# An order of work written as a table: VectorE's operations with two SBUF operands moved to PSUM, the score mask to ScalarE and GpSimd

## The reference, cut to what matters

```python
x = _layernorm(x + _L0_gnn_ref(x, adj, ...))   # attention, 12 heads, with an adjacency mask
x = _layernorm(x + _L1_gnn_ref(x, adj, ...))   # 2 graph convolutions
x = _layernorm(x + _L2_gnn_ref(x, adj, ...))   # 2 directed convolutions
x = _layernorm(x + _L3_gnn_ref(x, adj, ...))   # attention, 12 heads, adjacency as a bias
...
scores = scores + beta * adj_e
scores = jnp.where(adj_e > 0, scores, -9000000000000000.0)
probs = jax.nn.softmax(scores, axis=-1)
...
u = u_left * adj_tri + u_left * diag_mask + u_right * jnp.swapaxes(adj_tri, 1, 2)
delta_exp_u = jnp.exp(u) * adj
attention = delta_exp_u / (jnp.sum(delta_exp_u, axis=2, keepdims=True) + 1e-10)
```

## Time and profile before

| | |
|---|---|
| time, median of 3 runs | 2729.16 us (2726.61 to 2732.68) |
| profiled execution | 2730.39 us, span 2728.5 us |
| TensorE busy | 2582.3 us, 95% |
| VectorE busy | 2077.7 us, 76% |
| ScalarE busy | 2046.5 us, 75% |
| GpSimd busy | 2117.1 us, 78% |
| granted TensorE clock, mean | 0.986 |

### The profile page before, as it was taken

How to read it: one execution, slowest core, us unless ns; L and a number is a source line. 1 busy time by engine, 2 the same in 40 slices (tenths; PEclk the granted TensorE clock), 3 DMA queues, 4 the chain that set the end, 5 groups by cost and what they waited for, 6 DMA issues and landing times.

```text
span 2728.5 us, 90881 instructions
## 1 busy us (share of the span) xinstructions
PE 2582.3 (95%) x33728; PEld 1930.4 (71%) x33728; DVE 2077.7 (76%) x7848; ACT 2046.5 (75%) x5716; POOL 2117.1 (78%) x3211
## 2 busy tenths in 40 slices
PE   5899999999999999999999999999999999999995
PEld 4667777776777777777777777777777777777763
DVE  6677877777877777777777777777787777887774
ACT  6667777777777777777777777777777777787775
POOL 6577878778778788778787788888787787887774
PEclk9899999999999999999999999999999999999997
DMA  7734544445444544444454454444454544454433
GB/s 182 164 62 78 90 86 83 91 84 93 81 87 80 91 91 80 90 91 80 87 94 80 88 93 80 90 91 79 88 94 84 86 88 79 85 96 82 78 61 74
DMA packets 809952, 243.18 MB, mean 89 GB/s; under 512 B 768688, under 2 KB 808752, under 8 KB 809520
## 3 DMA queue, kind: packets, MB, share of 16 engines
q1 hardware_dynamic: 801056, 222.42, 45.5%
q10 hardware_dynamic: 8464, 14.94, 1.8%
HBM read 35.92 MB, written 12.58 MB: 18 GB/s over the span
## 4 chain that ended last, share of the span: by engine, by line
PE 45%; POOL 18%; DVE 16%; ACT 7%; DMA 6%; issue 6%; SPq 1%; DVEq 0%; POOLq 0%; ACTq 0%
PE bank L921 7%; PE bank L923 6%; PE bank L922 6%; PE bank L912 5%; PE bank L913 5%; PE bank L914 5%; DMA region<-region 5%; POOL region L717 3%; DVE region L1091 3%; POOL ab L733 3%; PE bank L995 3%; ACT region L832 2%; POOL region L706 2%; PE bank L951 2%; POOL region L733 2%
## 5 line engine op out<-in xcount | busy, mean ns | idle before, releaser
L912 PE MATMUL bank<-region,w_hi 128*128 128x128 f16 x3960 | 686.0, 220 | 35.0 <-DMA region<-region 25.0
L913 PE MATMUL bank<-region,w_hi 128*128 128x128 f16 x3960 | 685.6, 220 | 0.0
L914 PE MATMUL bank<-region,w_lo 128*128 128x128 f16 x3960 | 685.4, 220 | 0.0
L921 PE MATMUL bank<-w_hi,region 128*128 128x384 f16 x1815 | 593.9, 327 | 11.4 <-DMA region<-region 6.1
L923 PE MATMUL bank<-w_hi,region 128*128 128x384 f16 x1815 | 593.2, 327 | 0.0
L922 PE MATMUL bank<-w_lo,region 128*128 128x384 f16 x1815 | 593.1, 327 | 0.0
L717 POOL TENSOR_TENSOR region<-region 128x512 f16<-128x512 f32 x330 | 385.2, 1167 | 220.6 <-ACT region L838 219.2
L832 ACT ACTIVATE region<-region,small 128x128 f32<-128x128 f32 x1320 | 419.8, 390 | 133.1 <-DVE small L1091 73.2
L912 PEld LDWEIGHTS bank<-region,w_hi 128*128 128x128 f16 x3960 | 390.0, 98 | 63.3 <-issue 26.4
L1091 DVE CUSTOM_DVE_ANT_0 region<-bank,mask 128x128 f32<-128x128 f32 x1320 | 304.4, 285 | 134.5 <-PE bank L951 123.2
L913 PEld LDWEIGHTS bank<-region,w_hi 128*128 128x128 f16 x3960 | 389.9, 98 | 23.8 <-issue 16.5
(11 more groups left out here) (229 smaller groups left out, 7795.8 us busy)
## 6 DMA issues: line engine op xcount, KB each, us to landing
region<-region SPq DMA_TRANSPOSE x715, 3.1
last_unit<-w_dram ACTq DMA_DIRECT2D x19, 576.0 KB, 6.0
x<-x_dram SPq DMA_DIRECT2D x55, 192.0 KB, 2.5
out_dram<-region SPq DMA_DIRECT2D x55, 192.0 KB, 2.2
adj<-adj_dram SPq DMA_DIRECT2D x55, 64.0 KB, 2.3
mask<-adj_t_dram SPq DMA_DIRECT2D x55, 64.0 KB, 2.0
rows<-rows_dram ACTq DMA_DIRECT2D x5, 576.0 KB, 4.3
last_unit<-last_unit SPq DMA_TRANSPOSE x117, 3.1
```

The source lines that it names most:

```text
L912: pe.matmul(dst, lhsT=w_hi[:, w, k, cols], rhs=t_hi[u][:, k, :], start=(k == 0), stop=False)
L913: pe.matmul(dst, lhsT=w_hi[:, w, k, cols], rhs=t_lo[u][:, k, :], start=False, stop=False)
L914: last = pe.matmul(dst, lhsT=w_lo[:, w, k, cols], rhs=t_hi[u][:, k, :], start=False, stop=(k == DT - 1))
L921: pe.matmul(dst, lhsT=t_hi[u][:, k, :], rhs=w_hi[:, w, k, :], start=(k == 0), stop=False)
```

## The change

No instruction of VectorE reads two operands from SBUF any more, the preparation of the weights aside. `masks` is split: ScalarE multiplies the adjacency by minus beta, GpSimd makes the barred entries and adds both. `divide` keeps its inverse in the PSUM bank of the last `attend` (attend 2 or 5), the first attention's quotient lies there too, and `residual` 0 reads it from there; so this bank is held until `residual` 0 or `divide` 1. `u_gcn` multiplies its halves one by one, the second in its bank, and adds from there. A small denominator of `inner` moves to the bank as well. `PARTS`, `SHIFTED` and `PERIOD` have new numbers throughout, so that all lists and banks change.

```diff
-PERIOD = 20.1080
+PERIOD = 20.0041
...
-    (VECTOR, "masks", 0): (2.743, 0.600, 0.900, ((SYNC, "load", 0),), ()),
+    (POOL, "masks", 0): (-115.045, 1.020, 1.100, ((SCALAR, "masks", 0),), ()),
+    (SCALAR, "masks", 0): (-94.836, 0.190, 0.300, ((SYNC, "load", 0),), ()),
...
-           "scores": lambda s: (VECTOR, "scores", s), "attend": lambda s: (SCALAR, "attend", s),
+           "scores": lambda s: (VECTOR, "scores", s), "attend": lambda s: {DT - 1: (VECTOR, "residual", 0), 2 * DT - 1: (VECTOR, "divide", 1)}.get(s, (SCALAR, "attend", s)),
...
-        u_pair = [a[:, 0:2 * N].rearrange("p (a n) -> p a n", n=N) for a in score_at]
+        u_left = [a[:, 0:N] for a in score_at]
...
         def inner_of(i, k):
+        def denom_of(made):
+            return made[:, PD - 1:PD]
...
+            def masks(i, k):
+                u = i % UNITS
+                pool.wait_ge(*loaded.at(i, "in"))
+                pool.tensor_scalar(score[u][:, 3, :], adj[u], 0.0, -MASKED, ALU.is_le, ALU.mult).then_inc(gpsimd_done.of(i), 1)
+                pool.wait_ge(*gpsimd_done.at(i, "barred"))
+                pool.wait_ge(*scalar_done.at(i, "minus beta"))
+                pool.tensor_tensor(mask_bias[u], mask_bias[u], score[u][:, 3, :], ALU.add).then_inc(gpsimd_done.of(i), 1)
...
+            def masks(i, k):
+                u = i % UNITS
+                if (k, i) == first(SCALAR, "masks"):
+                    act.wait_ge(beta_loaded, 16)
+                    act.activation(minus_beta[:, :], beta[:, :], ACT.Copy, scale=-1.0).then_inc(minus_beta_made, 1)
+                    act.wait_ge(minus_beta_made, 1)
+                act.wait_ge(*loaded.at(i, "in"))
+                act.activation(mask_bias[u], adj[u], ACT.Copy, scale=minus_beta[:, 0:1]).then_inc(scalar_done.of(i), 1)
...
+                    elif read_by == "divide":
+                        pe.wait_ge(*mixed_out.at(j, "o", n))
...
-            def masks(i, k):
-                u = i % UNITS
-                if (k, i) == first(VECTOR, "masks"):
-                    dve.wait_ge(beta_loaded, 16)
-                    dve.tensor_scalar(minus_beta[:, :], beta[:, :], -1.0, None, ALU.mult).then_inc(minus_beta_made, 1)
-                    dve.wait_ge(minus_beta_made, 1)
-                dve.wait_ge(*loaded.at(i, "in"))
-                dve.tensor_scalar(mask_bias[u], adj[u], 0.0, -MASKED, ALU.is_le, ALU.mult).then_inc(numbers.of(i), 1)
-                dve.wait_ge(*numbers.at(i, "mask"))
-                dve.scalar_tensor_tensor(mask_bias[u], adj[u], minus_beta[:, 0:1], mask_bias[u], ALU.mult, ALU.add)\
-                   .then_inc(numbers.of(i), 1)
...
             def scores(i, s):
-                    dve.wait_ge(*numbers.at(i, "mask and beta"))
+                    dve.wait_ge(*gpsimd_done.at(i, "mask"))
...
             def divide(i, k):
+                held = bank("attend", DT * k + DT - 1, i)
+                inverse = held[:, PD - 2 * H:PD - H]
+                dve.wait_ge(*max((scalar_done.at(i, "o", DT * k + t) for t in range(DT)), key=lambda at: at[1]))
+                dve.reciprocal(inverse, o_un[u][:, :, HD]).then_inc(numbers.of(i), 1)
+                    not_low = held[:, PD - H:PD]
-                    dve.tensor_scalar(flag[u], low[u], 0.0, None, ALU.not_equal).then_inc(numbers.of(i), 1)
+                    dve.tensor_scalar(not_low, low[u], 0.0, None, ALU.not_equal).then_inc(numbers.of(i), 1)
-                    dve.scalar_tensor_tensor(flag[u], top[u], 0.0, flag[u], ALU.not_equal, ALU.max).then_inc(numbers.of(i), 1)
-                dve.wait_ge(*max((scalar_done.at(i, "o", DT * k + t) for t in range(DT)), key=lambda at: at[1]))
-                dve.reciprocal(inv[u], o_un[u][:, :, HD]).then_inc(numbers.of(i), 1)
-                if k:
-                    dve.wait_ge(*numbers.at(i, "inverse", k))
-                    dve.tensor_tensor(inv[u], inv[u], flag[u], ALU.mult).then_inc(numbers.of(i), 1)
+                    dve.scalar_tensor_tensor(flag[u], top[u], 0.0, not_low, ALU.not_equal, ALU.max).then_inc(numbers.of(i), 1)
+                    dve.wait_ge(*numbers.at(i, "row is not 0", k))
+                    dve.tensor_tensor(inverse, inverse, flag[u], ALU.mult).then_inc(numbers.of(i), 1)
-                dve.tensor_tensor(o[u].rearrange("p (h c) -> p h c", c=HD), o_un[u][:, :, 0:HD],
-                                  inv[u].unsqueeze(2).broadcast_to([128, H, HD]), ALU.mult).then_inc(mixed_out.of(i), 1)
+                dst = o[u] if k else held[:, 0:D]
+                dve.tensor_tensor(dst.rearrange("p (h c) -> p h c", c=HD), o_un[u][:, :, 0:HD],
+                                  inverse.unsqueeze(2).broadcast_to([128, H, HD]), ALU.mult).then_inc(mixed_out.of(i), 1)
             def u_gcn(i, layer):
-                dve.tensor_tensor(u_pair[u], bank("u_gcn", layer, i)[:, 0:2 * N].rearrange("p (a n) -> p a n", n=N), mask_pair[u], ALU.mult)\
-                   .then_inc(numbers.of(i), 1)
-                dve.wait_ge(*numbers.at(i, "masked", layer))
-                dve.tensor_tensor(e_of(i, "u_gcn", layer), u_pair[u][:, 0, :], u_pair[u][:, 1, :], ALU.add).then_inc(mixed_out.of(i), 1)
+                left, right = (bank("u_gcn", layer, i)[:, n * N:(n + 1) * N] for n in range(2))
+                dve.tensor_tensor(u_left[u], left, mask_pair[u][:, 0, :], ALU.mult).then_inc(numbers.of(i), 1)
+                dve.tensor_tensor(right, right, mask_pair[u][:, 1, :], ALU.mult).then_inc(numbers.of(i), 1)
+                dve.wait_ge(*numbers.at(i, "right masked", layer))
+                dve.tensor_tensor(e_of(i, "u_gcn", layer), right, u_left[u], ALU.add).then_inc(mixed_out.of(i), 1)
...
-                dve.tensor_scalar(col(u, DENOM3), made[:, D:D + 1], 1e-10, 1e-3, ALU.add, ALU.mult).then_inc(numbers.of(i), 1)
+                dve.tensor_scalar(denom_of(made), made[:, D:D + 1], 1e-10, 1e-3, ALU.add, ALU.mult).then_inc(numbers.of(i), 1)
...
-                    dve.scalar_tensor_tensor(col(u, BASE), col(u, ROOT), float(np.sqrt(D / (D - 1.0))), col(u, DENOM3),
+                    dve.scalar_tensor_tensor(col(u, BASE), col(u, ROOT), float(np.sqrt(D / (D - 1.0))), denom_of(bank("mix", k, i)),
...
-                    dve.scalar_tensor_tensor(z[u], o[u], 1.0, x[u], ALU.mult, ALU.add, accum_out=col(u, SUM)).then_inc(mixed_out.of(i), 1)
+                    dve.scalar_tensor_tensor(z[u], bank("attend", DT - 1, i)[:, 0:D], 1.0, x[u], ALU.mult, ALU.add, accum_out=col(u, SUM)).then_inc(mixed_out.of(i), 1)
```

More of the change, by code:

```diff
@@ new lines @@
+    (SYNC, "scores", 5): (-138.238, 1.240, 4.000, ((POOL, "scores", 5), (PE, "attend", 4)), ()),
+    (SCALAR, "turn", 5): (-130.888, 0.413, 0.600, ((SCALAR, "norm", 2),), ()),
+    (SCALAR, "turn", 0): (-128.905, 0.412, 0.600, ((SYNC, "load", 0),), ()),
+    (POOL, "bias", 8): (-125.896, 0.955, 1.090, ((SCALAR, "project", 8),), ()),
+    (POOL, "scores", 1): (-125.372, 1.150, 1.420, ((SCALAR, "scores", 1),), ()),
+    (PE, "project", 1): (-125.084, 1.513, 1.710, ((SYNC, "turn", 0),), ()),
+    (SCALAR, "spread", 0): (-124.915, 0.830, 0.950, ((VECTOR, "residual", 0),), ()),
@@ new lines @@
+    (SYNC, "turn", 3): (-58.717, 1.240, 3.600, ((POOL, "turn", 3),), ()),
+    (SCALAR, "project", 16): (-57.963, 0.370, 0.570, ((PE, "project", 16),), ()),
+    (SCALAR, "project", 9): (-57.614, 0.370, 0.570, ((PE, "project", 9),), ()),
+    (VECTOR, "residual", 1): (-56.044, 0.480, 0.620, ((VECTOR, "gain", 1),), ()),
+    (PE, "attend", 5): (-54.144, 0.330, 0.520, ((SYNC, "scores", 5),), ()),
+    (SCALAR, "u_di", 0): (-53.564, 0.342, 0.674, ((VECTOR, "u_di", 0),), ()),
+    (SYNC, "load_adj", 0): (-53.517, 0.450, 2.500, ((VECTOR, "scores", 2),), ()),
@@ new lines @@
+    (SCALAR, "turn", 4): (-26.620, 0.412, 0.600, ((VECTOR, "gain", 2),), ()),
+    (POOL, "bias", 14): (-25.462, 0.955, 1.090, ((SCALAR, "project", 14),), ()),
+    (SYNC, "turn", 5): (-25.409, 1.240, 3.600, ((POOL, "turn", 5),), ()),
+    (POOL, "bias", 13): (-24.530, 0.955, 1.090, ((SCALAR, "project", 13),), ()),
+    (VECTOR, "delta_gcn", 1): (-23.350, 0.199, 0.407, ((SCALAR, "u_gcn", 1),), ()),
+    (SCALAR, "spread", 2): (-23.140, 0.830, 0.950, ((VECTOR, "residual", 2),), ()),
+    (SCALAR, "project", 7): (-21.486, 0.371, 0.570, ((PE, "project", 7),), ()),
@@ L1210, in _ @@
             for name, k, i in sequence(VECTOR):
[L1211 removed]
+                {"weight": weight, "add_bias": add_bias, "turn": turn, "project": project,
                  "scores": scores, "divide": divide, "u_gcn": u_gcn, "delta_gcn": delta_gcn, "u_di": u_di,
```

371 lines of the change are left out of this document (174 added, 197 removed), and 60 rows, old and new, of the table SHIFTED.

## The result

The kernel after takes 2687.5 us (median of four, 2686.6 to 2692.7) against 2730.6 for the kernel before beside it: ratio 0.985, 95% interval 0.983 to 0.987, so 1.5% faster. The prediction was 2681, with a range of 2643 to 2727 (2655 to 2705 for the case it held likeliest). The profiled span is 2686.4 us.

The account below looks back on a forecast made before the run. TensorE bounds the kernel, busy 2582 of 2728.5 us, so only its idle time can pay. Terms -58 + 21 - 5 - 6 = -48 take 2729 to 2681 us, range 2643 to 2727.

Parts of the forecast that it names:

- The four kinds of waits, -58: TensorE's waits at mix 0, project 3, attend 1 and scores 5 go: 1.0 us a unit over 58 units, 58 us.
- Scores 3, +21: Scores 3 reuses banks of scores 0 too soon after it, so TensorE waits 0.5 us in 41 units: +21 us.
- Others, -5 (bounds -20 and +25): TensorE's other waits shrink a little, while mix 2 and mix 3 have less room but fit: net -5 us.
- more comes back: Rival, chance 0.16: held VectorE or GpSimd also caused TensorE's other waits; 30 us more idle time goes, giving 2651 us.
- Worth nothing by itself, VectorE being 75% busy.: VectorE's 1.8 us less work a unit counts only where TensorE waits.
- GpSimd's 1.1 us, covered: GpSimd's two added masks operations, at most 544 ns each, 1.1 us a unit, stand far ahead of the scores they feed.
- The slower rival: Rival, chance 0.12: masks on GpSimd make bias 9 and 12 late, so mix 2 and mix 3 wait: +75 us, 2756.
- ScalarE, 261 ns: ScalarE gets one more activation of 128 columns for masks, taking 261 ns like L869.
- VectorE, -1.8 a unit: VectorE's work falls 1.8 us of 32.5 a unit, through masks, division and convolution; small operations taken as nothing.
- the 2685: Time in us that the skill's rule of slower PSUM operands on VectorE would leave, in place of 2681.
- Head 0, end -6: First 120 us unchanged (bounds -8 and +8); the stretch after the last mix nets -6 us (bounds -12 and +8).

Follow-up runs that it names:

- finer_release: Kernel after, orders kept: TensorE waits only for reads of the scores banks it takes over, the bank taken soonest being read first; 2672.6 us, 0.978 of before.
- masks_thrice: Kernel after with GpSimd's first operation of masks done three times in place of once; 2783.1 us, 1.019 of before.

## Why the prediction was right, step by step

- **The four kinds of waits, -58.** Place and cause were right: per unit they had cost 1.1 us (I said 1.0), and all four are gone. For attend 1 and scores 5 masks alone is enough, in the old order too; mix 0, which the prediction put to masks as well, needs u_gcn out of SBUF too. That their going would be worth its full price was wrong by itself: in the old order 5 us were left of it, 10 with u_gcn, since other waits followed.
- **Scores 3, +21.** Right in mechanism and near in size: 34 of 40 units wait, (11.5 + 2.1) / 34 = 0.40 us each on the list, 0.13 more under the drawn ends, 0.45 a unit. Less the 0.09 that scores 3 lost in the kernel before too, it is 0.40 for the 0.5 forecast, 16 us. In the case shown u_di's last matmul starts at 1384.40, scores 3 could follow 0.06 later and starts at 1385.02: 0.56 late. finer_release, which takes one read of VectorE (0.29 us) out of it, confirms it.
- **Others, -5 (bounds -20 and +25).** Two errors that cancelled, which is luck. By the time lost in front of each part, both kernels laid out alike, scores 0 and project 1 went from 0.12 to 0.46 us a unit, which I did not foresee; I had looked at mix 2 and mix 3, where nothing came. And the parts that neither this nor the two terms above name fell from 0.89 to 0.60, for which I had 0.1: the rival *more comes back* was half true.
- **"Worth nothing by itself, VectorE being 75% busy."** This is the step that failed. With the order of after kept, masks on VectorE cost 46 us, up to 19 of them by the lower clock, and the divisions and u_gcn in SBUF 34. I held the greater distances of the new order to be what removed the waits, and priced the operations by VectorE's busy time. Yet the new order is the one that needs them most. GpSimd has long blocks without a gap in both (the longest of each unit 17 us in the mean before, 19 after, gaps under 0.15 us left aside), but only in the new one does TensorE wait at the end of one: in front of scores 0 it loses 0.08 us a unit before, 0.26 after, 0.49 with only masks moved, 1.26 with all old operations. The step should have been: how much room has the part at the end of such a block, and which held operation stands ahead of it.
- **GpSimd's 1.1 us, covered.** Its size was right in sum (664 + 457 ns, though 544 was called the most for each), its cover was not: 10 us. The listing showed the bias and a turn behind masks; five parts further on stood `low`, which I did not follow. The slower rival had the right engine and the wrong place; masks_thrice shows that with 1.3 us more it would have come true.
- **ScalarE, 261 ns.** Its activation takes 395 ns. L869 of the kernel before reads and writes PSUM with plain numbers as scale and bias; the new one reads and writes SBUF, with a column of SBUF as scale. Two rows of after stand between: 328 ns in PSUM with a column (L895, which also adds up its row), 390 ns from SBUF to SBUF with a column (L844). So at most 66 ns are the column's, and at least 62 the place of the operands, if the two add up. The Trainium skill, "ScalarE: Activation LUTs", section "What ACT_TABLE_LOAD costs", gives 186 ns + 0.833 ns a column and 93 ns more for each operand that is a column, by its figures an estimated 293 + 93 = 386; the total of 395 is near it, but these rows put less than 93 on the column.
- **VectorE, -1.8 a unit.** Measured -2.5. (Its part for masks reads -1.3 in the prediction; 589 + 800 is 1.39, and with that the sum is the 1.8 that it gives.) By part, in summed durations, masks are 1.4 less, u_gcn 0.06; `divide` is 0.70 less in place of 0.32, and `gain`, which reads the moved denominator, 0.26 and residual 0.16, for which the sum had nothing: the small operations and residual 0 were held too. That PSUM costs more, as "VectorE: DVE Perf Modes" of the Trainium skill has it in its section on the TRN2 errata, is not seen: the shortest, unheld L1123 of the kernel before took 299 ns with both operands in SBUF, and L1138 with one in PSUM has a mean of 299. Nothing here bears out the 2685 that the prediction drew from that rule, for which it shows no working.
- **Head 0, end -6.** Head +2. From the last mix on 67.7 us (60.7 before, guessed 63, and 68 was named as a sign of being wrong): ScalarE's 47.4 us were as forecast, the edges longer. With what TensorE had no longer to do before, the end still won 10 us, some 4 of them because TensorE is at 1.2 GHz for 32 us there in place of 40.

The sum by stretches: +2 in the first 120 us, -16 up to 800, -19 up to 2400, -10 at the end: -43. The forecast terms come to (58 - 21 + 5) / 58 = 0.72 us a unit. In the stretch whose rows were read, 39.4 units, that is 28 us, and 19 came. Between 120 and 800, where the price was only carried over, it is 12, and 16 came; the end gave 4 more than forecast. That the total lies within 5 us of the forecast's -48 is in part luck.

## What to carry to other kernels

An order that is written down is worth what it is only with the durations for which it was made: test the operations in the old order and the order with the old operations before either gets the credit. Here the operations won in both orders, the order only with them. The slack of an engine is read at the part that others wait for, behind the work that stands ahead of it without a gap, not from the idle share of its span. And where a planner's table has one number for "result is there" and another engine uses it as "buffer is free" (0.42 against 1.1 us for scores), that is where the new order puts things too close; waiting for the one bank that is needed gave half of that back. Where a wait is long, the work behind it has to be looked at too: the 1.28 us added to GpSimd cost 1.65 a unit, some of it by TensorE's lower clock.
